# One strided operation in place of two for adding keys and values to their edge rows in a graph attention kernel

## What is computed

```python
q = (x @ Wq + bq).reshape(n, H, C)
k = (x @ Wk + bk).reshape(n, H, C)
v = (x @ Wv + bv).reshape(n, H, C)
e = (edge_attr @ We).reshape(-1, H, C)
kj = k[src] + e
vj = v[src] + e
logits = jnp.einsum('ehc,ehc->eh', q[dst], kj) / np.sqrt(C)
ex = jnp.exp(logits - segment_max(logits, dst)[dst])
a = ex / (segment_sum(ex, dst)[dst] + 1e-16)
agg = segment_sum(vj * a[:, :, None], dst)
```

## Time and profile before

| what | value |
|---|---|
| median of 3 runs | 4827.84 us (4825.83 to 4828.0) |
| the profiled execution | 4832.06 us |
| its span, first to last instruction | 4830.3 us |
| pass e1, about | 1355 to 2960 us of the span |
| pass e2, about | 3116 to 4700 us of the span |

### The profile page before, as it was taken

The page is one execution under the profiler, slowest core; times in us unless marked ns, Lnnn a source line. Parts: engine busy times, 40 slices in busy tenths (PEclk is TensorE's granted clock), DMA queues, the critical chain, the costliest instruction groups (busy, mean ns, idle before and its releaser), DMA issues. The chain is left out here.

```text
span 4830.3 us, 107746 instructions
## 1 busy us (share of the span) xinstructions
PE 4189.2 (87%) x17694; PEld 3210.6 (66%) x17694; DVE 3989.0 (83%) x22772; ACT 2982.2 (62%) x10607; POOL 3116.4 (65%) x2996
## 2 busy tenths in 40 slices
PE   2887887888979999999999998889999999999988
PEld 2766666675547777777777774567777777777755
DVE  4655555556869999999999998789999999999986
ACT  1111111112319898989898984149999999989971
POOL 6677777740067777777777771287777777777730
PEclk9999999999999999999999999999999999999989
DMA  4666666654568887878788773587777777777734
GB/s 121 189 192 196 192 193 193 191 167 149 169 212 237 233 236 232 233 229 236 231 234 228 231 230 104 173 247 231 226 230 228 231 228 227 226 228 231 226 114 149
DMA packets 663064, 996.73 MB, mean 206 GB/s; under 512 B 99667, under 2 KB 489690, under 8 KB 662407
## 3 DMA queue, kind: packets, MB, share of 16 engines
q0 software_dynamic: 171408, 540.40, 38.1%
q1 hardware_dynamic: 491000, 449.44, 30.8%
HBM read 870.01 MB, written 119.44 MB: 205 GB/s over the span
## 5 line engine op out<-in xcount | busy, mean ns | idle before, releaser
L1303 POOL DMA_INDIRECT e_kv<-kv,src x1664 | 1635.0, 983 | 748.1 <-DVE e_kvj L1420 449.7
L1571 ACT ACTIVATE e_vals<-e_kvj,e_ex 128x65 f32<-128x65 f32 x6572 | 1725.1, 334 | 5.5 <-PE e_sum L1366 5.1
L1366 PE MATMUL e_sum<-e_vals,e_mask 128*128 128x260 f32 x3328 | 1063.7, 403 | 206.2 <-ACT e_vals L1571 190.0
L1325 PE MATMUL e_q<-q,e_pick 128*128 x3328 | 1017.2, 387 | 95.3 <-DVE e_logit L1428 66.4
L1428 DVE CUSTOM_DVE_ANT_0 e_kvj<-e_kvj,e_q 128x64 f32<-128x64 f32 x6656 | 1060.2, 214 | 3.4 <-PE e_q L1325 2.2
L152 POOL DMA_INDIRECT e_x<-x_rows,e_src x783 | 747.3, 954 | 263.1 <-issue 172.3
L1366 PEld LDWEIGHTS e_sum<-e_vals,e_mask 128*128 128x128 f32 x3328 | 563.0, 190 | 454.4 <-issue 379.7
L1325 PEld LDWEIGHTS e_q<-q,e_pick 128*128 128x128 f32 x3328 | 618.2, 191 | 252.4 <-issue 169.9
L1315 PE MATMUL e_e<-e_we,e_ea 112*128 112x256 f32 x2496 | 752.3, 382 | 17.4 <-DMA e_ea<-attr_tiles 16.2
L1316 PE MATMUL e_e<-e_we,e_ea 112*128 112x256 f32 x2496 | 745.8, 380 | 0.0
L1510 DVE TENSOR_TENSOR acc<-acc,e_sum 128x260 f32 x1664 | 697.3, 419 | 41.4 <-issue 23.6
(11 more groups left out here) (223 smaller groups left out, 4479.1 us busy)
## 6 DMA issues: line engine op xcount, KB each, us to landing
e_ea<-attr_tiles SPq DMA_DIRECT2D x1248, 112.0 KB
edges<-q SPq DMA_DIRECT2D x208, 256.0 KB
e_spots<-locals SPq DMA_DIRECT2D x416, 128.0 KB
e_made<-edges SPq DMA_DIRECT2D x416, 128.0 KB
e_kv<-kv,src POOLq DMA_INDIRECT x1664
kv<-n_proj_rows SPq DMA_DIRECT2D x98, 256.0 KB
q<-attr_tiles SPq DMA_DIRECT2D x208, 112.0 KB
n_x<-x_rows SPq DMA_DIRECT2D x98, 128.0 KB
```

The costliest lines, as they stand in the source:

```text
L1303: e.indirect_dma_start(out=kv[:, u, :], out_offset=None, **rows_of(kv_rows, k["src"][:, i:i + 1])).then_inc(kv_got[u], 16)
L1325: e.matmul(pe_q[i % 2][:, 0:D], pick[:, c, at:at + P], rows, start=True, stop=True).then_inc(q_done, 1)
L1366: e.matmul(sums[n % 2][:, 0:VALS], mask[:, n % R, :], vals[:, n % R, :], start=True, stop=True).then_inc(summed, 1)
L1571: by_weight = e.activation(vals[:, n % R, h * HV:(h + 1) * HV], kvj[:, 2 + n % NV, h, :], ACT.Copy, scale=ex[:, b % 2, h, r:r + 1])
```

## The change

The two adds of a step become one. Its target is a slice of kvj that takes the key slot and the value slot by a step between them, its first input is the whole gathered row read as two halves, and its second input is the edge row read twice, by a dimension of stride 0. The wait for weighed now stands ahead of the joint add. One semaphore, kvj_done, takes the place of kj_done and vj_done, for all who waited for either.

```diff
@@ vector engine, logits(i)
                     e.wait_ge(kv_got[i % NG], 16 * (i // NG + 1))
+                    key_at, value_at = i % 2, 2 + i % NV
...
                     if i >= 2:
                         e.wait_ge(dots_done, i - 1)
-                    e.tensor_tensor(kvj[:, i % 2, :, 0:C], kv[:, i % NG, 0:D].rearrange("p (h c) -> p h c", h=H), edge,
-                                    ALU.add).then_inc(kj_done, 1)
                     if i >= NV:
                         e.wait_ge(weighed, i - NV + 1)
-                    e.tensor_tensor(kvj[:, 2 + i % NV, :, 0:C], kv[:, i % NG, D:].rearrange("p (h c) -> p h c", h=H), edge,
-                                    ALU.add).then_inc(vj_done, 1)
-                    e.wait_ge(kj_done, i + 1)
+                    e.tensor_tensor(kvj[:, key_at:value_at + 1:value_at - key_at, :, 0:C],
+                                    kv[:, i % NG, :].rearrange("p (a h c) -> p a h c", a=2, h=H),
+                                    edge.unsqueeze(1).to_broadcast([P, 2, H, C]), ALU.add).then_inc(kvj_done, 1)
+                    e.wait_ge(kvj_done, i + 1)
                     e.wait_ge(q_done, i + 1)
@@ sync, load_made(c)
-                        e.wait_ge(vj_done, (c - 1) * QUAD)
+                        e.wait_ge(kvj_done, (c - 1) * QUAD)
@@ gpsimd, the gather of step i
-                        e.wait_ge(vj_done, i - NG + 1)
+                        e.wait_ge(kvj_done, i - NG + 1)
@@ tensor, edge_product(a)
-                        e.wait_ge(vj_done, step_of(a - 2) + 1)
+                        e.wait_ge(kvj_done, step_of(a - 2) + 1)
```

More of the change, by code:

```diff
@@ L1185, in edge_pass_attention @@
         w_got, cleared, ones_set = ph.sem("w_got"), ph.sem("cleared"), ph.sem("ones_set")
-        e_done, q_done, kj_done, vj_done, dots_done, picked, apart_done = (
-            ph.sem(n) for n in ("e_done", "q_done", "kj_done", "vj_done", "dots_done", "picked", "apart_done"))
+        e_done, q_done, kvj_done, dots_done, picked, apart_done = (
+            ph.sem(n) for n in ("e_done", "q_done", "kvj_done", "dots_done", "picked", "apart_done"))
         flat_done, lr_done, fw_done, mx_inner = (ph.sem(n) for n in ("flat_done", "lr_done", "fw_done", "mx_inner"))
```

## The result

The changed kernel took 4901.73 us in the median of 4 runs (4898.5 to 4912.17) and the kernel before 4826.84 us. The ratio is 1.0162, with a 95% interval of 1.0143 to 1.0182: 75 us slower, where +65 had been forecast. The profile is of an execution of 4912.17 us.

What follows compares the result with a forecast made beforehand. DVE was taken to bound the two attention passes, 94% busy. Terms 72 + 13 - 20 = +65 us gave 4893 us against the median, +1.3%, with 4862 to 4930 us for 8 in 10.

Steps and rivals of the forecast that it cites:

- DVE's plain step: From start of adds to first dot: 0.71 us in place of 0.667, 0.043 more a step, +72 us over 1664 steps.
- The joint add's 675 ns: Duration of the one 512-element add on DVE that replaces two of 256: 0.675 us, ends 0.67 and 0.68.
- hand-over: First dot, waiting for the add directly ahead, starts 0.035 us after its end; such a wait costs about 0.12 us.
- Strides and the repeated operand: Operand form of the joint add: costed at nothing; for the repeated operand 40 us more is the end.
- issue: DVE's waits for instruction issue: one instruction, wait and signal fewer each step, counted as nothing.
- The moved wait: Wait for weighed ahead of the joint add: 0.2 us a batch, 64 batches, +13 us (nothing to 63).
- the absorption: DVE's waits for PE at block product and key add shrink by half: -20 us (0 to -39).
- the passes nearly all pay or gain: In the two attention passes DVE is 94% busy, so what its step costs more or less nearly all reaches the time.
- DVE's busy time: Falls or stays while the kernel slows: adds total 1123 us in place of 1371, with a 35 ns idle gap.
- Rival A: At the first dot: the hand-over does not show, step 0.077 us shorter, PE then bounds; 4753 us; chance 0.07.
- Rival B: In the passes, PE and ACT take up all of DVE's extra time: no change, 4828 us; chance 0.05.
- Rival C: DVE's wait for ACT binds at three places a batch, 0.33 us each: 4963 us; or repeated operand, 4933; chance 0.08.

Runs made afterwards that it cites:

- before_load_early: The kernel before, with DVE's register load for the sums asked for ahead of the key add; 4827.54 us, ratio 0.9998.
- hand_over: The kernel before, two adds, with only the first dot waiting for the value add in place of the key add; 4960.33 us, ratio 1.0274.
- wait_early: The kernel before, two adds, with only the wait for weighed moved ahead of the key add; 4828.76 us, ratio 1.0002.
- sum_between: The changed kernel with DVE's sum put between joint add and dots, and the register load asked for ahead of the joint add; 4872.66 us, ratio 1.0087.
- both_no_merge: The kernel before, two adds, with the wait for weighed ahead of both and the first dot waiting for the value add; 4969.17 us, ratio 1.029.
- load_early: The changed kernel with DVE's register load for the sums asked for ahead of the joint add; 4880.63 us, ratio 1.0107.

## Why the prediction was right

**DVE's plain step** was foretold at 0.71 us to the first dot in place of 0.667, and measured at 0.712 in place of 0.663: +0.049, within the 0.035 to 0.055 given. The joint add's 675 ns were 680, and the hand-over's 0.035 us were 0.035. Strides and the repeated operand cost nothing, as forecast: 680 against the 682 of the earlier trace rows.

**What was missing.** Two costs on DVE stood in no term. The register load, of which the prediction counted nothing for issue, though the 24 us of it at the sum in the earlier trace rows were this load (before_load_early has 1.6): 416 x 0.09 = 37 us on DVE, 21 us of the time. And the four dots, 0.430 against 0.423 from first to last, 0.007 x 1664 = 12 us; they were slower by the same amount in hand_over. Together DVE's plain steps grew by 0.049 x 1664 + 37 + 12 = 131 us, where 72 had been put down.

**What was absorbed** was therefore mis-sized as well. The moved wait had +13 and measured at nothing with two adds (wait_early, -3 to +5) and 9 beside the hand-over; the absorption had -20. The time grew by 75, so 56 of 131 us were taken up. Where, can be added up from the timelines of the two profiled executions: DVE's time from start to start, both passes from their first add to their last, in us.

| stretch of DVE's program | before | changed | difference |
|---|---|---|---|
| first add to first dot | 1139 | 1190 | +51 |
| the dots | 940 | 950 | +10 |
| up to the sum | 75 | 71 | -4 |
| softmax and block product | 346 | 326 | -20 |
| up to the next add | 568 | 609 | +41 |
| together | 3068 | 3146 | +78 |

To the first dot the plain steps alone would have made it 0.049 x 1664 = 82. The 31 us less are the value add's wait for ACT, which stood in this stretch before (wait_early takes 30 us out of it); it now stands ahead of the joint add with 58 us. So the moved wait is +27 on DVE, where the prediction had 13. The rest gave back: up to the sum 4 us net, which is 41 less than with the 37 of the register load; 20 at the softmax and the block product, whose waits for PE fell from 27.4 to 15.5; and 41 - 58, some -16, on the rest of the way to the next add, where waits for issue, for gathers and for PE are all a little shorter. The sum as measured is 82 + 10 + 27 - 4 - 20 - 16 = 79 (78 before rounding), against 72 + 13 - 20. Most of the register load's 37 us was thus no net cost in this count: the late sums only changed their steps, though taking them out gives 21 us.

The sentence that "the passes nearly all pay or gain" was too strong; 94% busy time did not mean that 94% of a loss arrives. In hand_over 133 of (0.114 + 0.007) x 1664 + 37 = 238 us arrived (its first dot starts at 0.777), of the merge 67 of 108, of the load 21 of 37 or 40 in the changed kernel, and none of 28 in the kernel before. That PE and ACT, which run at nearly the same pace, are the reason is argued from their busy time; the shares are measured, and they are not one constant. The errors had opposite signs, and the sum of 65 came near 75 partly by that, which is luck.

**DVE's busy time** was to fall or stay. It rose from 3989 to 4021 us. The sum of the adds fell from 1372 to 1131 us, but the page counts overlapped time once, and a step was covered throughout before.

**Rival A** named the right quantity. Uncovered, the hand-over costs more than merging gains. Covered, DVE's plain step does become shorter (1.50 us in sum_between, 1.56 before), but no kernel here turned that into time. The Trainium skill (page "VectorE: DVE Perf Modes", section "The DRAIN you can't avoid") says of eight chained copies that a semaphore after each costs nothing extra. For these additions hand_over disagrees: 0.45 us from start to start in place of 0.33, and 133 us. **Rival B** was nearer than its 0.05 suggests: not all, but 56 of 131 us, four tenths, were hidden. **Rival C**: DVE's idle time for ACT did rise, from 21 to 58 us, and in wait_early from 21 to 78 at no cost. With the joint add it may cost some 20 to 40 us; that stays open.

## What to carry to other kernels

Merging two operations saves the fixed part of one (here 0.065 us), but look at what reads the result: if it follows at once, the tail of the merged operation and the hand-over, which the second operation used to cover, are laid bare (here 0.12 us), along with whatever the engine's program has to do behind the waiting instruction. Merge where an independent operation can stay between, and make sure that this operation's own inputs are there in time; that this pays is not shown here, as the one operation that was tried (sum_between) waited for its inputs. Where several engines run at nearly one pace, expect only a part of a change on the busiest to arrive, here about six tenths in most comparisons and nothing in two (wait_early, before_load_early).

## What the runs showed of the hardware that was not expected

A register load from SBUF in a vector program (each fourth step) did not show in six tenths of the steps of the kernel before that have one (0.14 us from the last dot to the sum). It showed with 0.09 us a time once a wait for the engine's own result stood four dot products ahead of it, and with some 0.3 us in steps of the kernel before in which an add had waited, as in the earlier trace rows (0.45 us from dot to sum). Asking for it ahead of the joint add removed it there (4902 to 4881 us). The four dot products became 2% slower from first to last, 0.430 against 0.423 us, in each kernel in which the first one waits for the operation directly ahead (the changed kernel, hand_over, both_no_merge, load_early). In sum_between, where the sum stands between, they take 0.423 again in the median (0.427 in the mean). Why was not tried.
